# Fast-scheme products added up in TensorE's banks, with ScalarE's copies between them, and block sums of eight weight pieces moved into the second pair's groups

## The chip, the cores and the metric

One core of a Trainium2 chip runs the whole kernel. The metric is the device time of one execution in microseconds. The engines are TensorE (PE), VectorE (DVE), ScalarE (ACT), GpSimd (POOL) and SyncE (SP), which here issues most DMAs. Each has its own queue, works through it in the order written, and waits on semaphores.

## The reference

```
xn = layernorm(x)                          # x: 8 x 512 tokens x 512
q, k, v = xn @ Wq.T + bq, xn @ Wk.T + bk, xn @ Wv.T + bv
ctx = (elu(q)+1) * cumsum((elu(k)+1) * v, over tokens) * 32**-0.5
s = ctx @ Wo.T + bo
u = fwht(xn * SU_ug) / 64                  # Walsh-Hadamard transform over 512
h = silu(u @ W_gate.T * sg) * (u @ W_up.T * su)     # 2048 wide
f = fwht(h * SU_dp) / 64 @ W_down.T * sd
out = x + s * silu(f)
```

## The kernel before

All matrices are split into an fp16 high and low half, and each product is made of three fp16 matmuls (high x high, high x low, low x high). The tokens come in 8 chunks of 512, worked on as 4 pairs of chunks. The weights of q, k, v, gate and up are cut into 22 pieces ("groups" g = 0 to 21): pieces 0 to 5 are K, V, Q, K, V, Q, then gate and up alternate. A group gives four tiles of 128x512: two blocks of output rows by the two chunks of the pair.

The first pair (p = 0) computes its tiles plainly, 12 matmuls each, while the other engines prepare the weights for the later pairs: `s_sums` (lines 1040 to 1043) and `s_low` (line 1053) on VectorE with `s_high` on ScalarE make the block sums S1 to S4 of a piece, GpSimd loads their blocks and stores them. `S_TILES` says after which tile of the first pair each piece's sums are made; the last three of the 22 are made between the first and the second pair. Down weights are transformed and stored in four slabs, the last in group 20.

Pairs 1 to 3 use a fast 2x2 scheme: 7 products of 6 matmuls in place of 8 (`group`, lines 1446 to 1457), each into a bank of its own. VectorE adds the banks to four tiles in SBUF with 7 additions (`add`, line 919), which begin from ScalarE's copy of the first product (`copy_p1`, line 660). The finished tiles are then used: for K and Q ScalarE makes exp and relu (lines 670, 673) and VectorE the feature (line 925), for Q also the context (line 949); V is multiplied and scanned by VectorE (lines 935, 940); gate gets a Silu (line 683); up is multiplied by it (line 958) and split into halves by ScalarE (`hidden_high`, line 690) and VectorE (`hidden_low`, line 967). SyncE loads each group's weights five loads ahead into a ring of 5 slots.

After the groups of a pair TensorE runs four down quads of 48 matmuls for each chunk (line 1522) and an out product of 48 (line 1553). Meanwhile VectorE takes the contexts' maxima (`ctx_absmax`, line 819), the next pair's layernorm statistics (line 829) once its tokens have been loaded over the freed tiles (`load_x`, which waits for the last `h_ready`), the normalised tokens (line 855, after GpSimd's rstd), splits the contexts (lines 997, 998) and makes the next pair's token sums and their halves (`x_sums`, `t_low`, line 898). The order is written out by hand on each engine:

```
# DVE, pairs 1 to 3
last_sums(p)
ctx_absmax(p)
ln_stats(p + 1); normalise_pair(p + 1)     # p < 3
ctx_scale(p); split_ctx(p, 0..7)
x_sums(p + 1, 0); t_low(p + 1, 0)          # p < 3
out_scale(); outputs(2 * p)
...
# PE, first out product of the pair, t == 0
pe.wait_ge(ctx_split, 8 * p + 8)
elif p < PAIRS - 1:
    pe.wait_ge(x_ready, 2 * p + 3 + cc)
```

## Time and profile before

| | |
|---|---|
| median of 3 runs | 1337.56 us (1337.24 to 1337.63) |
| profiled execution | 1335.45 us, its span 1333.6 us |
| granted TensorE clock | 0.999 of full speed (2.4 GHz) |
| TensorE busy | 1305.5 us, 98% of the span |
| VectorE busy | 1011.3 us, 76% |
| ScalarE busy | 457.8 us, 34% |
| GpSimd busy | 41.8 us, 3% |
| first pair | tiles to 298 us, down quads and out products to 406 us |
| groups of the later pairs | from 406, 715 and 1024 us, some 201 us each |

Busy time of TensorE counts matmuls that overlap once; its ends are modelled, so a small idle time can be hidden behind a matmul's end, and starts are the safer thing to count from. Times of single operations overlap in the same way on VectorE and ScalarE: the distance from start to start is shorter than the duration.

### The profile page before, as it was taken

What the parts mean: (1) busy time and instruction counts of PE and PEld (TensorE: products, weight loads), DVE (VectorE), ACT (ScalarE), POOL (GpSimd) and SP (SyncE); (2) the same over time, 40 slices, a digit from 0 to 9 for tenths busy, and PEclk for the clock granted to TensorE, in tenths of its full rate; (3) what the DMA queues carried; (4) which work ended last, traced back from release to release, by engine and by line L of the source; (5) the groups of instructions that cost most, each with busy time, mean ns of one, the idle gap of its engine ahead of it and who ended that gap; (6) DMA issues with size and microseconds to landing.
All of it is one profiled execution on the core that took longest, in us unless ns stands there. A gap on an engine that the chain in (4) does not pass through costs nothing. (4 is left out here: it accounts for less than half of the span.)

```text
span 1333.6 us, 16120 instructions
## 1 busy us (share of the span) xinstructions
PE 1305.5 (98%) x6100; PEld 597.9 (45%) x6100; DVE 1011.3 (76%) x1629; ACT 457.8 (34%) x683; POOL 41.8 (3%) x72
## 2 busy tenths in 40 slices
PE   5999999999999999999999999999999999999998
PEld 3444444444444444444444444444444444444443
DVE  6899999979648997777717998778734998778333
ACT  5945545541123443330113443332112433332000
POOL 0102000001000000000000000000000000000000
PEclk9999999999999999999999999999999999999999
DMA  9624555568264323325244323325244423323240
GB/s 375 246 79 166 198 212 198 180 254 293 94 236 158 127 97 124 127 99 186 97 156 158 127 98 124 126 101 184 95 158 142 143 100 121 127 107 115 95 126 32
DMA packets 47550, 199.39 MB, mean 150 GB/s; under 512 B 5105, under 2 KB 5361, under 8 KB 31985
## 3 DMA queue, kind: packets, MB, share of 16 engines
q1 hardware_dynamic: 41424, 176.87, 36.9%
q0 software_dynamic: 6048, 21.50, 4.4%
q8 instruction: 48, 0.79, 0.2%
q14 instruction: 30, 0.24, 0.1%
HBM read 153.26 MB, written 45.09 MB: 149 GB/s over the span
## 5 line engine op out<-in xcount | busy, mean ns | idle before, releaser
L1455 PE MATMUL bank<-xops,ring 128*128 128x512 f16 x2772 | 601.1, 380 | 3.2 <-DVE work L919 3.1
L1455 PEld LDWEIGHTS bank<-xops,ring 128*128 128x128 f16 x2772 | 269.4, 98 | 334.4 <-DVE work L919 11.3
L919 DVE TENSOR_TENSOR work<-bank,work 128x512 f32<-128x512 f32 x462 | 305.4, 685 | 91.5 <-PE bank L1455 83.9
L1522 PE MATMUL bank<-ring,h_all 128*128 128x512 f16 x1536 | 333.8, 379 | 0.6 <-DMA ring<-scr_d 0.6
L1370 PE MATMUL bank<-xops,ring 128*128 128x512 f16 x1056 | 237.2, 379 | 1.5 <-DVE xops L868 1.5
L1522 PEld LDWEIGHTS bank<-ring,h_all 128*128 128x128 f16 x1536 | 150.0, 98 | 180.9 <-DMA ring<-scr_d 1.1
L1370 PEld LDWEIGHTS bank<-xops,ring 128*128 128x128 f16 x1056 | 102.5, 98 | 140.4 <-issue 28.1
L690 ACT ACTIVATE h_all<-work 128x512 f16<-128x512 f32 x128 | 80.2, 627 | 204.3 <-DVE work L958 204.3
L1189 DVE TENSOR_TENSOR gate_g<-bank,row 128x512 f32<-128x512 f32 x32 | 21.4, 689 | 104.5 <-PE bank L1522 103.9
L740 ACT ACTIVATE gate_g<-gate_g 128x512 f32<-128x512 f32 x32 | 19.9, 630 | 202.9 <-DVE gate_g L1189 202.9
L967 DVE TENSOR_TENSOR h_all<-work,h_all 128x512 f16<-128x512 f32 x128 | 87.4, 685 | 0.4
L683 ACT ACTIVATE work<-work,gate_out 128x512 f32<-128x512 f32 x96 | 66.4, 715 | 54.4 <-DVE work L919 54.4
L1553 PE MATMUL bank<-ring,ctx 128*128 128x512 f16 x384 | 84.2, 379 | 0.4 <-DVE xops L898 0.2
L958 DVE SCALAR_TENSOR_TENSOR work<-work,up_out 128x512 f32<-128x512 f32 x96 | 71.3, 743 | 0.0
L670 ACT ACTIVATE work<-work,vec,i_attn 128x512 f32<-128x512 f32 x48 | 38.8, 808 | 75.9 <-DVE work L919 75.9
L1553 PEld LDWEIGHTS bank<-ring,ctx 128*128 128x128 f16 x384 | 37.4, 98 | 46.2 <-issue 1.3
L660 ACT ACTIVATE work<-bank 128x512 f32<-128x512 f32 x66 | 38.7, 586 | 56.1 <-PE bank L1455 55.9
L925 DVE SCALAR_TENSOR_TENSOR work<-work 128x512 f32<-128x512 f32 x64 | 44.1, 689 | 13.7 <-ACT work L673 12.6
L631 ACT ACTIVATE ring<-ring 128x1024 f16<-128x1024 f32 x16 | 16.9, 1053 | 81.1 <-DVE ring L1043 78.0
L573 ACT ACTIVATE work<-bank 128x512 f32<-128x512 f32 x6 | 3.6, 597 | 112.6 <-PE bank L1482 112.6
L940 DVE TENSOR_TENSOR_SCAN work<-work 128x512 f32<-128x512 f32 x32 | 39.2, 1224 | 1.1
L673 ACT ACTIVATE work<-work,vec,i_attn 128x512 f32<-128x512 f32 x48 | 38.3, 799 | 0.0
(158 smaller groups left out, 835.6 us busy)
## 6 DMA issues: line engine op xcount, KB each, us to landing
ring<-scr_g SPq DMA_DIRECT2D x66, 1024.0 KB, 4.8
ring<-scr_d SPq DMA_DIRECT2D x32, 1024.0 KB, 4.8
scr_g<-ring SPq DMA_DIRECT2D x22, 512.0 KB, 3.5
scr_g<-ring POOLq DMA_DIRECT2D x22, 512.0 KB, 3.5
h_all<-in_ug_t SPq DMA_DIRECT2D x8, 1024.0 KB, 13.9
ring<-scr_f POOLq DMA_DIRECT2D x16, 512.0 KB, 3.7
x_res<-in_x SPq DMA_DIRECT2D x32, 256.0 KB, 3.5
out<-x_res SPq DMA_DIRECT2D x32, 256.0 KB, 6.8
```

Of the source, the lines that this page charges most:

```text
L670: act.activation(exp_tile(n), src, ACT.Exp, bias=vec[:, b + f:b + f + 1], scale=i_attn[:, m:m + 1])
L683: act.activation(tile(g, j), src, ACT.Silu, scale=gate_out[:, at:at + 1]).then_inc(act_tiles, 1)
L690: act.activation(h[:, i, TILE_OF[j], HI, :], tile(g, j), ACT.Copy).then_inc(h_hi, 1)
L919: dve.tensor_tensor(tile(g, to), bank[product][:, :], tile(g, other), ALU.add).then_inc(summed, 1)
L925: dve.scalar_tensor_tensor(tile(g, j), exp_tile(n), 1.0, tile(g, j), ALU.min, ALU.add) \
L940: dve.tensor_tensor_scan(tile(g, j), tile(g, j), tile(g, j), 0.0, ALU.add, ALU.bypass) \
L958: dve.scalar_tensor_tensor(tile(g, j), src, up_out[:, at:at + 1], tile(g - 1, j), ALU.mult, ALU.mult).then_inc(h_made, 1)
L967: dve.tensor_tensor(at[:, LO, :], tile(g, j), at[:, HI, :], ALU.subtract).then_inc(h_ready, 1)
L1370: mm = pe.matmul(plain_bank(g, j)[:, :], at[:, s, 2 * dh + kk, r, :], xops[:, kk, xs, PLAIN_B[dh][c], :], start=(n == 0), stop=(n == len(t ...
L1455: mm = pe.matmul(bank[n][:, :], weight_of(slot, s, b, kk), xops[:, kk, xs, c, :], start=(a == 0), stop=(a == 5))
L1522: mm = pe.matmul(bank[D_BANK[t]][:, :], at[:, s, cols], w[:, :, ws, :], start=(a == 0 and b == 0 and n == 0), stop=(a == KB - 1 and b == K ...
L1553: mm = pe.matmul(bank[R_BANK[t]][:, :], at[:, s, cols], o_weight(slot)[:, f, ws, :], start=(n == 0), stop=(n == 3 * KB - 1))
```

## The change

In pairs 1 to 3 the products of a group that belong to one sum are added by TensorE itself, because it goes on writing to the same bank. P1, P6, P7 and P4 go one after another into a "chain" bank; after each of the first three ScalarE copies the partial sum to a tile (`copy_sum`), and after the fourth the bank holds tile C21, which its user reads from the bank. P5 and then P3 share a "left" bank, P2 has a "right" bank. VectorE adds 3 times (`add`), one copy and one bank each. TensorE's order is interleaved over neighbouring groups (`group_order`), and in the last group of a pair 24 matmuls of the first down quad come ahead of the last two products and 24 behind them.

The tiles' order in a group is now C11, C22, C21, C12, and chunks, rows and plain banks of the first pair are renumbered with it. The block sums of pieces 14 to 21 are made in groups 6 to 13 of the second pair (`late_sums`; GpSimd loads and stores them, in a part of `h_all` that is free then); the first pair makes 14 at other tiles of its order.

```diff
 S1, S2, S3, S4, A11, A12, A22 = range(7)
-PRODUCTS = ((A11, B11), (S2, T2), (S3, T3), (S1, T1), (A12, B21), (S4, B22), (A22, T4))
+P1, P6, P7, P4, P5, P3, P2 = range(7)
+FACTORS = ((A11, B11), (S2, T2), (S3, T3), (A22, T4), (S1, T1), (S4, B22), (A12, B21))
+CHAIN_BANKS, LEFT_BANKS, RIGHT_BANKS = (0, 1), (2, 3), (4, 5)
...
+S_TILES = (2, 6, 10) + tuple(4 * g + 1 for g in range(8, 19))
 S_EARLY = len(S_TILES)
+S_LATE_FROM = 6
...
+def group_order(g):
+
+    if g == 0:
+        return [(0, P1), (0, P2), (0, P6), (0, P5), (0, P7), (1, P1)]
+    head = [(g - 1, P4), (g, P6), (g - 1, P3), (g, P2), (g, P7)]
+    if g < GROUPS - 1:
+        return head + [(g + 1, P1), (g, P5)]
+    return head + [(g, P5), (g, P4), (g, P3)]
+
+
+ORDER = [at for g in range(GROUPS) for at in group_order(g)]
+
+
+def products_to(p, g, m):
+
+    return len(ORDER) * (p - 1) + ORDER.index((g, m)) + 1
+
+def late_sums(g):
+
+    n = S_EARLY + g - S_LATE_FROM
+    return n if S_EARLY <= n < GROUPS else None
...
-            eng.wait_ge(summed, 7 * nth(p, g) + (3, 5, 6, 7)[j])
+            if j == C21:
+                eng.wait_ge(product_done, products_to(p, g, P4))
+                return chain_bank(g)[:, :]
+            eng.wait_ge(summed, 3 * nth(p, g) + (1, 2, 0, 3)[j])
...
-                    sp.wait_ge(product_done, 7 * nth(p, n) + 7)
+                    sp.wait_ge(product_done, products_to(p, n, P3))
...
-                    sp.wait_ge(s_stored, 16 * GROUPS)
+                    sp.wait_ge(s_stored, 16 * S_EARLY)
                     for s in range(3):
                         sp.wait_ge(piece_stored[s], 16 * len(range(s, GROUPS, 3)))
+                if p == 1 and S_EARLY <= n < GROUPS:
+                    sp.wait_ge(s_stored, 16 * (n + 1))
...
-                if n > S_OWN:
+                if n == S_EARLY:
+                    pool.wait_ge(quad_done, 2 * KB)
+                elif n > S_OWN:
                     pool.wait_ge(s_summed, n)
...
-                if n == S_EARLY + 1:
                     rstd_of(1)
+                    load_blocks(S_EARLY)
...
-            def copy_p1(p, g):
-
-                act.wait_ge(product_done, 7 * nth(p, g) + 1)
-                wait_free(act, p, g, SEED_TILE)
-                act.activation(tile(g, SEED_TILE), bank[0][:, :], ACT.Copy).then_inc(p1_copied, 1)
+            def copy_sum(p, g, n):
+
+                j = (C11, C12, C22)[n]
+                act.wait_ge(product_done, products_to(p, g, (P1, P6, P7)[n]))
+                wait_free(act, p, g, j)
+                act.activation(tile(g, j), chain_bank(g)[:, :], ACT.Copy).then_inc(copied, 1)
...
             def group(p, g):
+                if g == 0:
+                    copy_sum(p, g, 0)
+                elif kind_of(g - 1) != IS_UP:
+                    take(p, g - 1, C22)
+                copy_sum(p, g, 1)
+                if g and kind_of(g - 1) == IS_UP:
+                    take(p, g - 1, C22)
                 if g:
-                    take(p, g - 1, 2)
-                copy_p1(p, g)
+                    take(p, g - 1, C21)
+                copy_sum(p, g, 2)
+                if g + 1 < GROUPS:
+                    copy_sum(p, g + 1, 0)
+                if p == 1 and late_sums(g - 1) is not None:
+                    s_high(late_sums(g - 1))
                 if g:
-                    take(p, g - 1, 3)
-                take(p, g, 0)
-                take(p, g, 1)
+                    take(p, g - 1, C12)
+                take(p, g, C11)
...
-            s_high(S_EARLY)
             o_high()
-            s_high(S_EARLY + 1)
             silu_outs(0)
             x_high(1, 0)
             t_high(1, 0)
-            s_high(S_EARLY + 2)
...
+            def add(p, g, j):
+
+                at, m = ((right_bank(g), P2), (left_bank(g), P5), None, (left_bank(g), P3))[j]
+                dve.wait_ge(product_done, products_to(p, g, m))
+                dve.wait_ge(copied, 3 * nth(p, g) + (1, 3, 0, 2)[j])
+                dve.tensor_tensor(tile(g, j), at[:, :], tile(g, j), ALU.add).then_inc(summed, 1)
...
             def group(p, g):
                 if g:
-                    add(p, g - 1, 6)
-                    use(p, g - 1, 2)
-                    hidden_low(p, g - 1, 1)
-                add(p, g, 0)
+                    use(p, g - 1, C22)
+                    hidden_low(p, g - 1, C11)
+                    use(p, g - 1, C21)
+                    hidden_low(p, g - 1, C22)
+                    add(p, g - 1, C12)
+                add(p, g, C11)
                 if g:
-                    use(p, g - 1, 3)
-                    hidden_low(p, g - 1, 2)
-                add(p, g, 1)
+                    use(p, g - 1, C12)
+                    hidden_low(p, g - 1, C21)
+                add(p, g, C22)
                 if g:
-                    hidden_low(p, g - 1, 3)
-                add(p, g, 2)
-                add(p, g, 3)
-                add(p, g, 4)
-                use(p, g, 0)
-                add(p, g, 5)
-                use(p, g, 1)
-                hidden_low(p, g, 0)
+                    hidden_low(p, g - 1, C12)
+                use(p, g, C11)
+                if p == 1 and late_sums(g - 1) is not None:
+                    s_low(late_sums(g - 1))
+                if p == 1 and late_sums(g) is not None:
+                    s_sums(late_sums(g))
 
             def last_sums(p):
-                add(p, GROUPS - 1, 6)
-                use(p, GROUPS - 1, 2)
-                hidden_low(p, GROUPS - 1, 1)
-                use(p, GROUPS - 1, 3)
-                hidden_low(p, GROUPS - 1, 2)
-                hidden_low(p, GROUPS - 1, 3)
+                g = GROUPS - 1
+                use(p, g, C22)
+                hidden_low(p, g, C11)
+                use(p, g, C21)
+                hidden_low(p, g, C22)
+                add(p, g, C12)
+                use(p, g, C12)
+                hidden_low(p, g, C21)
+                hidden_low(p, g, C12)
...
-            s_sums(S_EARLY)
...
-            s_sums(S_EARLY + 1)
             for n in range(4, 8):
...
+            def wait_bank(p, g, m):
+
+                if m == P1:
+                    if g >= 2:
+                        wait_taken(pe, p, g - 2, C21)
+                    else:
+                        pe.wait_ge(z_ready, 8 * p - 4 + (2, 3)[g])
+                elif m in (P6, P7, P4):
+                    pe.wait_ge(copied, 3 * nth(p, g) + (P6, P7, P4).index(m) + 1)
+                elif m == P5:
+                    if g >= 2:
+                        pe.wait_ge(summed, 3 * nth(p, g - 2) + 3)
+                    elif g == 1:
+                        pe.wait_ge(o_read, 8 * p - 4 + 1)
+                    else:
+                        pe.wait_ge(z_ready, 8 * p - 4 + 4)
+                elif m == P3:
+                    pe.wait_ge(summed, 3 * nth(p, g) + 2)
+                elif g >= 2:
+                    pe.wait_ge(summed, 3 * nth(p, g - 2) + 1)
+                else:
+                    pe.wait_ge(o_read, 8 * p - 4 + (2, 3)[g])
+
+            def product(p, g, m):
+                slot = slot_of(p, g)
+                if m == P1:
+                    pe.wait_ge(slot_loaded[slot], 16 * loads_into(p, g))
+                    if g == 0:
+                        pe.wait_ge(x_ready, 2 * p + 2)
+                wait_bank(p, g, m)
+                to = chain_bank(g) if m in (P1, P6, P7, P4) else right_bank(g) if m == P2 else left_bank(g)
+                b, c = FACTORS[m]
+                terms = [(kk, s, xs) for kk in range(2) for s, xs in ((HI, HI), (HI, LO), (LO, HI))]
+                for a, (kk, s, xs) in enumerate(terms):
+                    mm = pe.matmul(to[:, :], weight_of(slot, s, b, kk), xops[:, kk, xs, c, :],
+                                   start=(a == 0 and m in (P1, P2, P5)), stop=(a == 5),
+                                   skip_group_check=True)
...
+            def group(p, g):
 
                 if g == 0:
-                    if n < 3:
-                        pe.wait_ge(z_ready, 8 * p - 4 + n + 2)
-                    else:
-                        pe.wait_ge(o_read, 8 * p - 4 + n - 2)
-                elif n == 0:
-                    pe.wait_ge(p1_copied, nth(p, g))
+                    product(p, 0, P1)
+                    product(p, 0, P2)
+                    product(p, 0, P6)
+                    product(p, 0, P5)
+                    product(p, 0, P7)
                 else:
-                    pe.wait_ge(summed, 7 * nth(p, g - 1) + (1, 2, 4, 5, 6, 7)[n - 1])
-
-            def group(p, g):
-                slot = slot_of(p, g)
-                pe.wait_ge(slot_loaded[slot], 16 * loads_into(p, g))
-                if g == 0:
-                    pe.wait_ge(x_ready, 2 * p + 2)
-                for n, (b, c) in enumerate(PRODUCTS):
-                    wait_bank(p, g, n)
-                    terms = [(kk, s, xs) for kk in range(2) for s, xs in ((HI, HI), (HI, LO), (LO, HI))]
-                    for a, (kk, s, xs) in enumerate(terms):
-                        mm = pe.matmul(bank[n][:, :], weight_of(slot, s, b, kk), xops[:, kk, xs, c, :],
-                                       start=(a == 0), stop=(a == 5))
-                    mm.then_inc(product_done, 1)
+                    product(p, g - 1, P4)
+                    product(p, g, P6)
+                    product(p, g - 1, P3)
+                    product(p, g, P2)
+                    product(p, g, P7)
+                if g + 1 < GROUPS:
+                    product(p, g + 1, P1)
+                if g:
+                    product(p, g, P5)
+                if g + 1 == GROUPS:
+                    down_part(2 * p, 0, (0, 1))
+                    product(p, g, P4)
+                    product(p, g, P3)
+                    down_part(2 * p, 0, (2, 3))
...
-                    pe.wait_ge(summed, 7 * nth(p, GROUPS - 1) + t - 1)
-
-            def down_quad(c, a):
+                elif t == 0:
+                    pe.wait_ge(z_ready, 4 * c - 3)
+                elif t < 3:
+                    wait_taken(pe, p, GROUPS - 3 + t, C21)
+                else:
+                    pe.wait_ge(summed, 3 * nth(p, GROUPS - 2) + 3)
...
                 for a in range(KB):
-                    down_quad(2 * p, a)
+                    if a or not p:
+                        down_quad(2 * p, a)
                     if a == 2 and 0 < p < PAIRS - 1:
                         transposes(p + 1, 0)
```

## Rows read from the trace of the kernel before

**Rows 1.** The chain that ended last, in order of time: start us, us, what.
```profile
1276.83 41.44 PE bank L1522 x192
```

**Rows 2.** Each pair's groups (two of three): stretch, its length, busy by engine.
```profile
406.13:607.30 201.17, 200.21 (x926) 89.81 (x925) 167.04 (x255) 77.45 (x117) 0.00 (x0) 1.00 0.36 126
714.68:916.20 201.52, 200.20 (x926) 89.81 (x925) 167.03 (x255) 77.44 (x117) 0.00 (x0) 1.00 0.35 126
```

**Rows 3.** Timeline of TensorE, second pair, group 6: start us, us, engine, line.
```profile
778.75 2.55 PE L1455 MATMUL bank<-xops,ring 128*128 128x512 f16 x11 [0.51 <-DVE work L919]
```

**Rows 4.** TensorE's waits in the first pair: us in total, times, longest.
```profile
PE bank L1522 <- DMA ring<-scr_d: 0.6, 1, 0.6
```

**Rows 5.** Groups of VectorE in the first of these stretches: busy, mean ns, idle before.
```profile
L919 DVE TENSOR_TENSOR work<-bank,work 128x512 f32<-128x512 f32 x153 | 101.1, 685 | 30.4 <-PE bank L1455 28.0 <-issue 1.5
```

**Rows 6.** Groups of VectorE in the first pair, shapes apart.
```profile
L1053 DVE TENSOR_TENSOR ring<-ring 128x1024 f16<-128x1024 f32 x13 | 15.8, 1219 | 0.1
...
L1043 DVE TENSOR_TENSOR ring<-ring 128x256 f32<-128x256 f32 x16 | 6.8, 425 | 0.5
```

**Rows 7.** Timeline of TensorE, first product of a pair.
```profile
406.13 2.11 PE L1455 MATMUL bank<-xops,ring 128*128 128x512 f16 x9
```

**Rows 8.** Timeline of ScalarE, first groups of the same pair.
```profile
407.62 0.60 ACT L660 ACTIVATE work<-bank 128x512 f32<-128x512 f32 x1 [3.61 <-PE bank L1455]
408.24 1.28 ACT L670 ACT_TABLE_LOAD   x1
...
416.69 0.60 ACT L660 ACTIVATE work<-bank 128x512 f32<-128x512 f32 x1
417.18 0.80 ACT L670 ACTIVATE work<-work,vec,i_attn 128x512 f32<-128x512 f32 x1
417.89 0.80 ACT L673 ACTIVATE work<-work,vec,i_attn 128x512 f32<-128x512 f32 x1
```

**Rows 9.** Timeline of VectorE, group 5 (three additions, then V's tiles).
```profile
451.48 1.89 DVE L919 TENSOR_TENSOR work<-bank,work 128x512 f32<-128x512 f32 x3
...
455.78 0.74 DVE L935 SCALAR_TENSOR_TENSOR work<-work,bv_in 128x512 f32<-128x512 f32 x1
...
457.70 0.67 DVE L919 TENSOR_TENSOR work<-bank,work 128x512 f32<-128x512 f32 x1
```

**Rows 10.** Timeline of VectorE, Q's tiles.
```profile
465.73 0.69 DVE L925 SCALAR_TENSOR_TENSOR work<-work 128x512 f32<-128x512 f32 x1 [0.39 <-ACT work L673]
...
467.13 0.68 DVE L919 TENSOR_TENSOR work<-bank,work 128x512 f32<-128x512 f32 x1
```

**Rows 11.** Timeline at the end of that pair's groups, VectorE then ScalarE.
```profile
608.67 0.74 DVE L958 SCALAR_TENSOR_TENSOR work<-work,up_out 128x512 f32<-128x512 f32 x1
...
609.45 0.63 ACT L690 ACTIVATE h_all<-work 128x512 f16<-128x512 f32 x1 [1.23 <-DVE work L958]
```

**Rows 12.** Timeline of ScalarE in the first pair, first gate group.
```profile
98.66 1.28 ACT L683 ACT_TABLE_LOAD   x1
99.95 1.50 ACT L683 ACTIVATE work<-bank,gate_out 128x512 f32<-128x512 f32 x2
```

**Rows 13.** Timeline at the end of that pair's groups.
```profile
607.30 12.90 PE L1522 MATMUL bank<-ring,h_all 128*128 128x512 f16 x59
...
611.99 4.83 DVE L819 TENSOR_REDUCE ctx_max<-ctx 128x1 f32<-128x512 f32 x8
...
617.58 2.47 DVE L829 BATCH_NORM_STATS2 stats<-work 128x6 f32<-128x512 f32 x4 [0.57 <-DMA work<-in_x]
```

**Rows 14.** Timeline at that pair's first out product.
```profile
648.27 2.36 DVE L898 TENSOR_TENSOR xops<-work,xops 128x1024 f16<-128x1024 f32 x2 [1.45 <-ACT xops L580]
...
650.77 4.48 PE L1553 MATMUL bank<-ring,ctx 128*128 128x512 f16 x20
```

**Rows 15.** Timeline of TensorE, the next pair's first out product.
```profile
959.79 1.46 PE L1553 MATMUL bank<-ring,ctx 128*128 128x512 f16 x6 [0.24 <-DVE xops L898]
```

**Rows 16.** Timeline of VectorE between rows 13 and 14.
```profile
627.57 0.17 DVE L852 TENSOR_SCALAR rstd<-rstd 128x8 f32<-128x8 f32 x1 [3.99 <-POOL rstd L485]
```

More of the change, by code:

```diff
@@ L81 @@
 DOWN_HIGH_AT, DOWN_LOW_AT = 14, 15
-S_TILES = (2, 6, 10) + tuple(4 * g + 1 for g in range(6, GROUPS))
+S_TILES = (2, 6, 10) + tuple(4 * g + 1 for g in range(8, 19))
 S_EARLY = len(S_TILES)
+S_LATE_FROM = 6
 S_OWN = 3
@@ L300, in plain_bank, with chain_bank, left_bank, right_bank @@
             return bank[PLAIN_BANKS[(4 * g + j) % len(PLAIN_BANKS)]]
+        def chain_bank(g):
+            return bank[CHAIN_BANKS[g % 2]]
+        def left_bank(g):
+            return bank[LEFT_BANKS[g % 2]]
+        def right_bank(g):
+            return bank[RIGHT_BANKS[g % 2]]
         def wait_taken(eng, p, g, j):
@@ L768, in _ @@
                     group(p, g)
-                take(p, GROUPS - 1, 2)
-                take(p, GROUPS - 1, 3)
+                for j in (C22, C21, C12):
+                    take(p, GROUPS - 1, j)
                 if p < PAIRS - 1:
@@ L1509, in down_quad @@
                 pe.wait_ge(slot_loaded[slot], 16 * loads)
[L1510 to L1525 removed]
+                for b in range(KB):
+                    k = KB * QUADS[a] + b
+                    i, r = k % 8, k // 8
+                    if cc == 0:
+                        pe.wait_ge(h_ready, 32 * p + 4 * i + 4)
+                    w, at = quad(slot)[:, :, b, :, :], h[:, i, 2 * r + cc, :, :]
+                    for t in ts:
+                        if a == 0 and b == 0:
+                            wait_down_bank(c, t)
+                        cols = slice(t * P, (t + 1) * P)
+                        for n, (s, ws) in enumerate(((HI, HI), (HI, LO), (LO, HI))):
+                            mm = pe.matmul(bank[D_BANK[t]][:, :], at[:, s, cols], w[:, :, ws, :],
+                                           start=(a == 0 and b == 0 and n == 0),
+                                           stop=(a == KB - 1 and b == KB - 1 and n == 2))
+                if ts[-1] == TB - 1:
+                    mm.then_inc(quad_done, 1)
+            def down_quad(c, a):
+                for ts in ((0, 1), (2, 3)) if a == 0 else ((0, 1, 2, 3),):
+                    down_part(c, a, ts)
             def out_product(c, t):
```

114 lines of the change are left out of this document (42 added, 72 removed).

## The prediction

> **What bounds the kernel now.** I read the page's busy shares first (the table above: TensorE nearly all of the span), then the chain that ended last. The chain's late part is TensorE alone, with 192 matmuls of 128x512 in 41.44 us [rows 1], so one takes 0.2158 us and one product of the fast scheme (6 matmuls) T = 1.295 us. The second view is the stretch of each pair's groups [rows 2]: 22 groups of 42 matmuls are 924 x 0.2158 = 199.43 us, and the stretches last 201.17, 201.52 and, in the last pair, as long as the first of them. So TensorE loses 1.74 + 2.09 + 1.74 = 5.6 us in all in the groups; the reader should see how small this is. Its timeline puts the losses in group 6, where TensorE waits for VectorE's additions of line 919 [rows 3]. That is where VectorE's debt from pieces 4 (V) and 5 (Q) comes due. In the first pair, from which the change takes block sums, TensorE's wait at the end is 0.6 us before the first down quad, and it is for a DMA, not for VectorE [rows 4]. The third place is the end of each pair, below.
>
> **What is removed.** Per group 7 additions become 3: 66 x 4 = 264 of 0.685 us [rows 5], 181 us of VectorE. It lies beside TensorE, except for the 5.6 us above. Eight block sums (four operations of 0.42 us, one of 1.22 us each [rows 6]) leave the first pair and the passage to the second. TensorE waits for none of them, so this is worth nothing: cover is TensorE's own work, and the 0.6 us before the quads hangs on the fourth down slab, whose stores follow its own tiles. In the second pair's groups 6 to 14 they cost VectorE 1.7 + 1.2 = 2.9 us a group. A gate group needs only its 3 additions (2.1 us), an up group 3 additions, 4 products of 0.74 and 4 subtractions (under 8 us), so the two average under 8 of 9.06 us, and the tightest point (the bank of C21, needed 5 T = 6.5 us into a group) just holds: 0.20 + addition 0.60 + product 0.66 + 1.13 + 1.6 of late sums + product 0.66 + subtraction 0.60 + product 0.74 = 6.2. Cost 0; if that cover is missing, about 0.3 us in each of four up groups. The pieces are stored some three groups before their loads; SyncE's new waits pass.
>
> **What is added: loops inside the groups.** The matmul count is the same, so TensorE's cost is only waits. Its order is now, per group g: P4(g-1), P6(g), P3(g-1), P2(g), P7(g), P1(g+1), P5(g). Each sum in a bank is copied by ScalarE before the next product goes on it, with two products (2.59 us) of cover. I walk the queues with these steps:
> - a product can be read 0.20 us after its slot ends (start 406.13, + 1.295, copy starts 407.62) [rows 7, 8];
> - ScalarE: copy to next 0.49, exp to relu 0.71, relu 0.80, exp+relu to the next 1.42; a table load 1.28 [rows 8];
> - VectorE: an addition or a plain product 0.69, but the next can start after 0.60 (three take 1.89); V's multiply and scan 1.92 together, the multiply alone 0.74 [rows 9]; Q's feature and context 1.40 together [rows 10];
> - a hand-over between engines 0.03 to 0.05 (608.67 + 0.74 = 609.41, and the copy starts at 609.45) [rows 11].
>
> K groups: ScalarE takes tile C12 of g-1 only after copying P1(g+1); VectorE adds C22 of g only after using that tile; P3(g) waits for it, due 3 T = 3.89 us after P1(g+1). The loop is 0.20 + 0.49 + 0.71 + 0.80 + 0.03 + 0.60 + 0.69 + 0.05 = 3.57: no loss.
> Q groups: the same with 1.40 for 0.60, that is 4.37: loss 0.48, twice a pair.
> V groups: VectorE's part starts at 2.23 of that loop (up to the feature), then 0.60 + 0.60 + 2 x 1.92 + 0.74 + 0.05 = 8.06 until C21 is taken from the bank; P1 of the group after next is due at 6 T = 7.77: loss 0.29, twice a pair.
> Group 1: ScalarE now copies P1(1) ahead of the pair's first exp, and the table load before that exp begins at 6 T + 0.20 + 0.60 = 8.57 us, after this copy, where it used to lie in an idle stretch. 8.57 + 1.28 + two tiles of 1.42 = 12.70, copy of P6(1) done at 13.33 with its hand-over; P7(1) is due at 10 T = 12.95: loss 0.38.
> Gate and up groups: copies come 1.3 to 1.8 us before need; no loss.
> Sum 0.38 + 2 x 0.48 + 2 x 0.29 = 1.9 a pair, 5.8 in all, against 5.6 now: **+0.2 us**. The debt that VectorE had goes, and ScalarE's place in the loops brings about as much back. Bounds: nothing (each wait hidden; -5.6) and twice my losses (+6.0); I take the walk, since each of its steps is a row.
>
> Whether more than the 1.28 us lies between a load and the work behind it shows in the first pair's first gate group: the load starts at 98.66 and the Silu at 99.95 [rows 12], so nothing follows. The Trainium skill (ScalarE: Activation LUTs, What ACT_TABLE_LOAD costs) says otherwise, a drain of about 1.38 us on top, 2.66 in all; by it group 1 would lose 1.76 instead of 0.38 us, and this sum would be 4.1 us higher. The trace does not agree with it.
>
> **What is moved: the end of each pair.** P4 and P3 of group 21 now come behind 24 matmuls of the first down quad. The last product thus ends 4 T = 5.18 us after the point E where the groups used to end, instead of at E. VectorE still goes through all of the last group's tiles before it starts the contexts' maxima (line 819), the next pair's statistics and the rest. Before: E = 607.30, maxima from 611.99, which is E + 4.69 [rows 13]. After: 5.18 + 0.20, the addition of C12 0.72, its product 0.74, hand-over 0.04, ScalarE's half 0.63 [rows 11], 0.03, and 0.60 to the next: E + 8.14. **3.45 us later.**
> Who waits for that? In the second and third pair VectorE makes the next pair's tokens (line 898) before TensorE may start the out product of line 1553. That chain is already what ends last: line 898 ends at 648.27 + 2.36 = 650.63 and line 1553 starts at 650.77 [rows 14]; one pair later the profile names line 898 as what TensorE waited for [rows 15]. Between the maxima and there VectorE has 38 us of work with two waits: 0.57 for the tokens' landing [rows 13] and 3.99 for GpSimd's rstd [rows 16]. Both move along, because the load is issued when the last hidden tile is done and rstd needs the statistics. So the delay arrives whole: 2 x 3.45 = **+6.9 us**. The last pair has no next tokens: its out product needs only split contexts, which would be ready near E + 25 and are due at E + 41.4, so 0. Bounds: 0, if those waits (4.6 us) swallowed it all, and 3.45 + 1.0 a pair, if the tokens' load, now closer behind the load of the out weights, landed 1 us later. I take 3.45.
> Starts of pairs: P2(0) now needs the second out tile read 1.3 us in instead of 5.2; VectorE reads it before the pair's first product starts, between the out products of that chunk. Cost 0.
>
> **Sum.** +0.2 + 6.9 = +7.1 us. The profiled execution took 1335.45 (span 1333.6, 1.8 around it), which gives 1342.6; the median is 2.1 above it, so 1337.56 + 7.1 = **1344.7 us**, 0.5% slower. Within 0.2% (2.7 us) a measurement of this kernel can't tell from no change.
>
> **Rivals.**
> A, my forecast: 1344.7, by itself 1342 to 1347. Chance 0.68.
> B, more waits inside the groups: the late sums of the second pair, or hand-overs a little longer in the V and Q loops, double my losses: +6 gives up to 1350; half of it 1347.7. For: the margins are 0.2 to 0.3 us. Against: the steps are measured. 0.08.
> B2, the table load before the pair's first exp holds ScalarE for as long again as its row says (1.28 us): group 1 loses 1.28 more, 3.8 in three pairs, 1348.5. For: two loads of the groups stand ahead of an idle stretch, where this wouldn't show. Against: [rows 12]. 0.04. This is the skill's rule of that page, which would put it at 1348.8.
> C, the groups lose nothing while the pair's end does: -5.6 + 6.9 gives 1338.9, within 0.2%. For: the loops may start from work that ScalarE did earlier. Against: copy and take stand in one queue. 0.12.
> E, the reordered end costs nothing: 1337.8. Against: [rows 14, 15]. 0.03.
> D, faster: TensorE is fed without a wait through the groups (-5.6), from VectorE's freed 181 us. It decides once the pair's end costs under 1.4 us a pair instead of 3.45; with none it gives 1332.0. For: the two waits inside the chain are longer than the delay. Against: both begin with work that is itself late. 0.05.
>
> **Chances and range.** Slower A + B + B2: 0.80; same C + E: 0.15; faster D: 0.05. The range takes in C's time and B's lower half: 1338.8 to 1348.0.
>
> **What the changed profile would show.** Right: additions x198, copies x198; TensorE's groups of pair 1 in about 201.3 us plus the 24 matmuls, with waits of 0.3 to 0.5 us for VectorE in groups 1 to 6 and none in group 6's old places; the maxima starting 8.1 us after E; the first out product of the second and third pair waiting 3.7 us for line 898's successor; none in the last pair; first pair unchanged to 0.2 us. Wrong: no wait ahead of those out products (then E or D), or groups above 203 us (B). Most dangerous for me are margins of tenths in the V and Q loops, and the assumption that VectorE's order at the pair's end has no slack.

## The result and the profile after

The changed kernel took 1351.94 us (median of 4 runs, 1349.76 to 1352.52), the kernel before beside it 1337.40 (1336.52 to 1337.63). The ratio is 1.0107 with a 95% interval of [1.0089, 1.0124]: 1.1% slower, some 14.5 us, where 7.1 us were forecast. The direction was right, the size was not, and 1351.94 lies above the range of 1338.8 to 1348.0. The profiled execution took 1349.76 us (span 1347.9), 14.3 us more than the one before.

The page gives the sizes. The additions fell to 198 and the copies rose to 198, as the diff says, and VectorE went from 76% to 63% of the span. TensorE's busy time rose by 5.6 us with the same 6100 matmuls, which waits alone don't explain. Columns of the groups: busy, mean ns of one, then the idle time before them and its releaser.
```profile
PE 1311.1 (97%) x6100; PEld 599.5 (44%) x6100; DVE 853.2 (63%) x1365; ACT 528.6 (39%) x815; POOL 46.6 (3%) x72
...
L972 DVE TENSOR_TENSOR work<-bank,work 128x512 f32<-128x512 f32 x198 | 134.2, 687 | 181.9 <-PE bank L1519 167.3
...
L1648 PE MATMUL bank<-ring,ctx 128*128 128x512 f16 x384 | 88.6, 393 | 7.5 <-DVE xops L961 7.5
```

TensorE's waits by releaser (us in total, times, longest) name the places. Line 1648 is the out product (line 1553 before) and line 961 the halves of the next pair's tokens (line 898 before).
```profile
PE bank L1648 <- DVE xops L961: 7.5, 2, 3.8
PE bank L1519 <- DVE work L972: 1.9, 6, 0.3
...
PE bank L1519 <- DVE work L1011: 1.5, 2, 1.1
...
PE bank L1519 <- DVE work L988: 1.2, 6, 0.2
...
PE bank L1519 <- ACT work L716: 0.7, 3, 0.2
```

**The pair's end.** TensorE's timeline in the first of the two (start, length, line, count), then VectorE's. The products of line 1519 end when the next line starts, at 614.60; the point E of the forecast is 4 T = 5.18 us ahead of that, 609.42. The maxima (line 882) start at 617.68 = E + 8.26, where they started at E + 4.69 [rows 13]: 3.57 us later. Both waits inside the chain move along (0.61 and 3.87, before 0.57 and 3.99 [rows 13, 16]), line 961 ends at 656.31, and TensorE, which had nothing left to do, starts at 656.45. In the kernel before it started without such a wait [rows 14].
```profile
606.83 5.34 PE L1612 MATMUL bank<-ring,h_all 128*128 128x512 f16 x24
612.01 2.75 PE L1519 MATMUL bank<-xops,ring 128*128 128x512 f16 x12
614.60 7.72 PE L1612 MATMUL bank<-ring,h_all 128*128 128x512 f16 x35
...
648.72 4.05 PE L1612 MATMUL bank<-ring,h_all 128*128 128x512 f16 x18
656.45 7.84 PE L1648 MATMUL bank<-ring,ctx 128*128 128x512 f16 x23 [3.68 <-DVE xops L961]
```
```profile
617.68 4.83 DVE L882 TENSOR_REDUCE ctx_max<-ctx 128x1 f32<-128x512 f32 x8
...
626.03 2.47 DVE L892 BATCH_NORM_STATS2 stats<-work 128x6 f32<-128x512 f32 x4 [0.61 <-DMA work<-in_x]
...
633.25 0.17 DVE L915 TENSOR_SCALAR rstd<-rstd 128x8 f32<-128x8 f32 x1 [3.87 <-POOL rstd L538]
...
653.95 2.36 DVE L961 TENSOR_TENSOR xops<-work,xops 128x1024 f16<-128x1024 f32 x2 [1.45 <-ACT xops L635]
```

**What stands behind the wait.** The windows around it (stretch, length, busy by engine, granted clock, DMA share, GB/s) show what the forecast did not have. Around a wait of 3.7 us the granted clock falls to half, 1.2 GHz, where it was 1.00 (2.4 GHz) in the 10 us up to 650: 14 matmuls in 5 us instead of 23, then 2.4 GHz again. By their starts 12 matmuls stand 0.427 us behind the one before instead of 0.216, and one 0.38, which is 2.7 us lost. One pair later, behind a wait of 3.79 us, it is 7 such matmuls and 1.7 us.
```profile
655.00:657.00 2.00, 0.55 (x2) 0.29 (x3) 1.97 (x4) 0.00 (x0) 0.00 (x0) 0.54 0.95 401
657.00:662.00 5.00, 5.00 (x14) 1.72 (x12) 0.98 (x3) 1.23 (x2) 0.00 (x0) 0.50 0.01 3
662.00:665.00 3.00, 3.00 (x16) 1.35 (x15) 2.36 (x4) 0.63 (x1) 0.00 (x0) 1.00 0.01 3
...
970.00:972.00 2.00, 0.10 (x1) 0.13 (x2) 1.97 (x4) 0.00 (x0) 0.00 (x0) 1.00 0.95 397
972.00:977.00 5.00, 5.00 (x16) 1.90 (x15) 1.83 (x3) 1.23 (x2) 0.00 (x0) 0.66 0.03 13
```
The Trainium skill (TensorE: Matmul & The Clock Gate, What's actually happening) says that the array's clock is gated to half after a stretch without work and let go by activity. The trace agrees, with the 0.50 behind the wait and the 1.00 that follows.

The fall does not coincide with the wait. The first time the clock is down before TensorE starts again at 656.45 (0.54 in the window from 655). The second time it is still at 1.00 up to 972.00, when TensorE has been working again since 971.90, and falls behind that.

**The groups.** From here on a wait is the distance between the starts of two matmuls beyond 0.216 us, worked out from the trace. Each pair loses 0.41 + 0.12 in group 1, 0.37 twice in the V groups and 0.49 twice in the Q groups, 2.25 us. The second pair loses 2.0 more around the late sums, 1.28 at 503.7 and 0.60 at 523.1. Together 8.8 us, against 5.5 in the same count of the trace before. (The row at 778.75 us in [rows 3] is of the third pair; the second has the like at 467 and 469 us.) In the second pair the groups take 609.42 - 405.73 = 203.7 us, above the 203 that the forecast had named as the sign of rival B.

ScalarE in group 1: the table load starts right behind the copy of P1(1), and TensorE waits until the copy at 418.46, as walked.
```profile
413.70 0.60 ACT L716 ACTIVATE work<-bank 128x512 f32<-128x512 f32 x1 [0.70 <-PE bank L1519]
414.32 1.28 ACT L726 ACT_TABLE_LOAD   x1
415.61 0.82 ACT L726 ACTIVATE work<-work,vec,i_attn 128x512 f32<-128x512 f32 x1
...
418.46 0.58 ACT L716 ACTIVATE work<-bank 128x512 f32<-128x512 f32 x1
```
```profile
405.73 13.11 PE L1519 MATMUL bank<-xops,ring 128*128 128x512 f16 x60
419.09 10.65 PE L1519 MATMUL bank<-xops,ring 128*128 128x512 f16 x48 [0.24 <-ACT work L716]
```

VectorE at the late sums of the second pair. It comes to them (line 1094) at 500.10 and stands until 501.32, because the piece's block has not landed. Its product of line 1011, which reads C21 from the bank, thus starts at 504.28 and ends at 505.02, and TensorE's next product waits for it until 505.17.
```profile
498.88 1.22 DVE L1107 TENSOR_TENSOR h_all<-h_all 128x1024 f16<-128x1024 f32 x1
501.32 0.42 DVE L1094 TENSOR_TENSOR h_all<-h_all 128x256 f32<-128x256 f32 x1 [1.22 <-DMA h_all<-scr_f]
...
504.28 0.74 DVE L1011 SCALAR_TENSOR_TENSOR work<-bank,up_out,work 128x512 f32<-128x512 f32 x1
```
```profile
505.17 18.29 PE L1519 MATMUL bank<-xops,ring 128*128 128x512 f16 x84 [1.12 <-DVE work L1011]
```
GpSimd issues this block's load at 493.26, only when the sums before it have read the shared buffer, and it lands 8.04 us later. The DMA issues from 455 to 545 us (KB each, median us to landing) give 6.9 us for such a load, beside ten loads of 1 MB by SyncE. In the first pair of the kernel before (120 to 200 us) the same 512 KB took 3.5 us. That SyncE's loads are the reason is likely, but no run tests it.
```profile
ring<-scr_g SPq DMA_DIRECT2D x10, 1024.0 KB, 6.3
h_all<-scr_f POOLq DMA_DIRECT2D x7, 512.0 KB, 6.9
```

**The balance** of the two profiled executions: groups +3.3 (8.8 less 5.5); out products +7.1 (3.85 + 3.96 less the 0.29 + 0.41 of before); half clock behind them +4.4 (2.7 + 1.7); start of the groups 0.4 earlier. The sum is +14.4, the spans differ by 14.3. Of the 0.4 the wait for the last down slab explains all: TensorE waited 0.58 us for it before and 0.18 now.

### The profile page after: what moved, and what is told of

Same layout as the page of the kernel before. It is cut to its first block, busy times and chain, and to the rows that moved or that the text cites. A ratio compares the mean times of both kernels' runs of the same rounds, so it can differ in the third digit from the quotient of the medians.

```text
span 1347.9 us, 16024 instructions
## 1 busy us (share of the span) xinstructions
PE 1311.1 (97%) x6100; PEld 599.5 (44%) x6100; DVE 853.2 (63%) x1365; ACT 528.6 (39%) x815; POOL 46.6 (3%) x72
## 4 chain that ended last, share of the span: by engine, by line
PE 77%; DVE 9%; ACT 4%; DMA 4%; issue 4%; SPq 0%; POOL 0%; DVEq 0%; ACTq 0%
PE bank L1519 35%; PE bank L1612 19%; PE bank L1421 13%; PE bank L1648 6%; PE bank L1454 2%; DMA h_all<-scr_f 2%; DMA work<-in_x 2%; ACT work L726 1%; ACT work L729 1%; PE bank L1465 1%; DVE work L988 1%; DVE ctx L1051 1%; DVE work L972 1%; DVE work L978 1%; DVE work L918 1%
## 5 line engine op out<-in xcount | busy, mean ns | idle before, releaser
L972 DVE TENSOR_TENSOR work<-bank,work 128x512 f32<-128x512 f32 x198 | 134.2, 687 | 181.9 <-PE bank L1519 167.3
L716 ACT ACTIVATE work<-bank 128x512 f32<-128x512 f32 x198 | 118.0, 596 | 244.8 <-PE bank L1519 244.8
L1648 PE MATMUL bank<-ring,ctx 128*128 128x512 f16 x384 | 88.6, 393 | 7.5 <-DVE xops L961 7.5
L1011 DVE SCALAR_TENSOR_TENSOR work<-bank,up_out,work 128x512 f32<-128x512 f32 x56 | 41.9, 748 | 24.6 <-PE bank L1519 11.4
L739 ACT ACTIVATE work<-work,gate_out 128x512 f32<-128x512 f32 x72 | 51.2, 717 | 5.4 <-DVE work L972 5.0
L1011 DVE SCALAR_TENSOR_TENSOR work<-work,up_out 128x512 f32<-128x512 f32 x72 | 51.9, 745 | 0.3
L628 ACT ACTIVATE work<-bank 128x512 f32<-128x512 f32 x6 | 3.6, 598 | 109.7 <-PE bank L1571 109.7
L739 ACT ACTIVATE work<-bank,gate_out 128x512 f32<-128x512 f32 x56 | 38.1, 681 | 21.2 <-PE bank L1421 21.1
L1252 DVE SCALAR_TENSOR_TENSOR s_f<-bank,o_out,row 128x512 f32<-128x512 f32 x32 | 23.9, 748 | 18.1 <-PE bank L1648 18.1
```

What stands on the lines that cost most here:

```text
L716: act.activation(tile(g, j), chain_bank(g)[:, :], ACT.Copy).then_inc(copied, 1)
L739: act.activation(tile(g, j), src, ACT.Silu, scale=gate_out[:, at:at + 1]).then_inc(act_tiles, 1)
L972: dve.tensor_tensor(tile(g, j), at[:, :], tile(g, j), ALU.add).then_inc(summed, 1)
L1011: dve.scalar_tensor_tensor(tile(g, j), src, up_out[:, at:at + 1], tile(g - 1, j), ALU.mult, ALU.mult).then_inc(h_made, 1)
L1648: mm = pe.matmul(bank[R_BANK[t]][:, :], at[:, s, cols], o_weight(slot)[:, f, ws, :], start=(n == 0), stop=(n == 3 * KB - 1))
```

## The experiments

Each was run beside the kernel before on the same chip; waits are of the profiled execution. e1 to e4 share one chip and its runs of the kernel before (1336.85, 13 runs), e6 to e9 another (1337.21, 9 runs).

One thing makes single executions differ, and it is no part of any edit. At 70 us, in the first pair, TensorE waits 1.9 to 2.5 us for VectorE in every trace. In those of e1, e2, e3, e4 and e8 some matmuls behind this wait run at half clock, in the others none do: from 73 to 78 us e8 has 13 matmuls at a mean granted clock of 0.67, e7 has 21 at 1.00, behind the same wait of 2.49 us. The groups of the second pair start at 406.9 to 408.8 us in the five, at 405.7 to 406.1 in the others (407.2 in e9, for a reason given there). So times within a trace are compared from the start or the end of its groups, and a single execution can lie 1 to 2 us off for this alone.

**e1_end_order**: the changed kernel with only the last group's order put back.
```diff
                 if g + 1 == GROUPS:
-                    down_part(2 * p, 0, (0, 1))
                     product(p, g, P4)
                     product(p, g, P3)
+                    down_part(2 * p, 0, (0, 1))
                     down_part(2 * p, 0, (2, 3))
```


> The changed kernel with P4 and P3 of group 21 right behind P5, both halves of the first down quad after them. Theory (the moved products hold VectorE up by 3.45 us, so TensorE stands 3.8 us before two out products, and its clock falls to half behind each): both waits go, no clock at half speed, 12 us less than the changed kernel, near 1339.7. Rival 1 (the half clock has its cause elsewhere, in the new order of the groups): waits go, half clock stays, near 1344. Rival 2 (the waits come from late tokens, from the closer load of the out weights): waits stay, no gain.

Measured 1337.07 us (1336.07 to 1338.08), ratio 1.0003 [0.9994, 1.0013]. Moving 24 matmuls past two products accounts for the whole loss. VectorE's and TensorE's timelines: the groups end at 609.83 and the maxima start 4.37 us behind that, where they started 8.26 us behind E; line 961 ends at 652.74, and line 1648 follows the down quads with no wait. No matmul there is at half clock.
```profile
614.20 4.83 DVE L882 TENSOR_REDUCE ctx_max<-ctx 128x1 f32<-128x512 f32 x8
...
650.38 2.36 DVE L961 TENSOR_TENSOR xops<-work,xops 128x1024 f16<-128x1024 f32 x2 [1.45 <-ACT xops L635]
```
```profile
653.01 3.19 PE L1648 MATMUL bank<-ring,ctx 128*128 128x512 f16 x14
```
The rest of the change, with group waits of 7.4 us against 5.5, is worth nothing that these runs can measure.

**e3_before_late_end**: the opposite, the moved matmuls alone in the kernel before (its down quad is split into parts as in the change).
```diff
                 for n, (b, c) in enumerate(PRODUCTS):
+                    if g == GROUPS - 1 and n == 5:
+                        down_part(2 * p, 0, (0, 1))
                     wait_bank(p, g, n)
...
                     mm.then_inc(product_done, 1)
+                if g == GROUPS - 1:
+                    down_part(2 * p, 0, (2, 3))
...
-                    down_quad(2 * p, a)
+                    if a or not p:
+                        down_quad(2 * p, a)
```


> The kernel before with only the moved end: 24 matmuls of the first down quad ahead of its last two products. Theory: the maxima start 4.6 us later than before (9.3 us after the old end of the groups), TensorE waits 4.9 us before two out products, the clock is at half speed after each: 9.2 us for the waits and 4 to 6 for the clock, 1350 to 1353. Rival 1 (half clock comes from something else in the changed kernel): 1346.6. Rival 2 (the groups' sums in the banks are what costs): 1338.

Measured 1353.20 us (1350.87 to 1354.60), ratio 1.0121 [1.0104, 1.0138]. One part of the change alone gives more than the whole loss. The waits were 5.89 and 5.66 us (longer than the 4.9 expected; here an addition and three tiles also lie behind the last two products, which may be the reason), and 25 matmuls ran at half clock, 5.3 us. Waits less before's 0.7 and the clock make +16.1; the medians differ by 16.4. The spans of the two profiled executions differ by 19.2, because in this one the groups also start 2.7 us later, the half clock in the first pair being one of the reasons. TensorE's timeline, then the windows:
```profile
659.08 6.09 PE L1561 MATMUL bank<-ring,ctx 128*128 128x512 f16 x15 [5.73 <-DVE xops L898]
```
```profile
659.00:664.00 5.00, 4.92 (x12) 1.75 (x13) 1.35 (x3) 1.23 (x2) 0.00 (x0) 0.50 0.00 0
```

**e2_two_raw**: the late sums get a second buffer for the loaded block, so that GpSimd loads one piece ahead.
```diff
-            return half_slot(3 + a) if n < S_EARLY else h_late[:, 2048 * a:2048 * a + 2048]
+            if n < S_EARLY:
+                return half_slot(3 + a)
+            part = 3 if a == 0 and (n - S_EARLY) % 2 else a
+            return h_late[:, 2048 * part:2048 * part + 2048]
...
+                elif n > S_EARLY:
+                    pool.wait_ge(s_summed, n - 1)
...
-                        .then_inc(s_loaded, 16)
+                        .then_inc(s_loaded if n < S_EARLY else s_late[(n - S_EARLY) % 2], 16)
```


> The changed kernel with two buffers for the blocks of the late sums, so each load is issued one group earlier. Theory (VectorE stands 1.2 and 0.6 us for a load that takes 6.9 us and was issued only after the previous sums, and hands the bank of C21 over late): the TensorE waits of 1.28 and 0.60 us in groups 10 and 12 of the second pair go, 1.9 us less, near 1350. Rival (the late sums' own 2.9 us a group on VectorE are too much in an up group): waits stay at 0.3 us or more in each up group.

Measured 1348.77 us (1347.83 to 1349.23), ratio 1.0089 [1.0074, 1.0104]. VectorE's timeline shows the sums (now line 1102) starting right behind line 1115 of the piece before, with no wait for the block (each buffer has a semaphore of its own for its loads):
```profile
499.97 1.22 DVE L1115 TENSOR_TENSOR h_all<-h_all 128x1024 f16<-128x1024 f32 x1
501.29 0.43 DVE L1102 TENSOR_TENSOR h_all<-h_all 128x256 f32<-128x256 f32 x1
```
TensorE's two waits there became 0.17 and 0.07 us. The mechanism is thus right, but its size is loose: the same code of the late sums cost TensorE 0.8 us in all in e1, 1.1 in e4 and e5 and 1.3 in e6, against 2.0 in the changed kernel and 0.4 here. The ratio's interval overlaps that of the changed kernel.

**e4_loops**: for K, V, Q and gate tiles ScalarE takes C12 ahead of its second copy, and VectorE adds C12 ahead of using C21.
```diff
+                if g and kind_of(g - 1) != IS_UP:
+                    take(p, g - 1, C12)
                 copy_sum(p, g, 2)
...
-                if g:
+                if g and kind_of(g - 1) == IS_UP:
                     take(p, g - 1, C12)
...
+                    if kind_of(g - 1) != IS_UP:
+                        add(p, g - 1, C12)
                     use(p, g - 1, C21)
                     hidden_low(p, g - 1, C22)
-                    add(p, g - 1, C12)
+                    if kind_of(g - 1) == IS_UP:
+                        add(p, g - 1, C12)
```


> The changed kernel, where for K, V, Q and gate groups VectorE adds C12 before it uses C21, and ScalarE takes C12 before it copies the sum after P7 (up groups as they were). Theory (two loops through ScalarE's and VectorE's order cost 0.49 us per Q group and 0.37 per V group): those four waits a pair go, 5.2 us less, near 1346.7; the 0.53 us of group 1 stay. Rival (TensorE waits because sums in a bank can't be read at once): the same waits at the same places, 1351.9.

Measured 1345.82 us (1344.28 to 1347.12), ratio 1.0067 [1.0052, 1.0082]. The V and Q waits are gone from all pairs, those of group 1 stay: behind the one at 420.60 TensorE's timeline has 275 matmuls in one piece.
```profile
420.60 59.64 PE L1524 MATMUL bank<-xops,ring 128*128 128x512 f16 x275 [0.23 <-ACT work L716]
```
The out products still waited 4.31 and 4.59 us, with 17 matmuls at half clock.

**e5_table** (one execution, no interval): an exp of one column at the start of a pair, so that the table is loaded in ScalarE's idle stretch.
```diff
                 if g == 0:
+                    act.wait_ge(halves_set, 1)
+                    act.activation(spare[:, 0:1], minus_half[:, 0:1], ACT.Exp)
                     copy_sum(p, g, 0)
```


> The changed kernel with only the one-column Exp ahead of each pair's first copy. Theory (the table load behind the copy of P1 of group 1 makes the copy of P6 late): the waits of 0.41 and 0.12 us in group 1 of each pair go, all others stay; some 1.6 us less, which one time can't show, so the waits in the trace decide. Rival (group 1 waits for the adding of the first group's tiles): the waits stay.

It took 1346.91 us beside 1338.53 for the kernel before. ScalarE's timeline shows the load moved from 414.32 to 403.85 and the first exp right behind the copy; TensorE's shows group 1 without a wait, as far as the first V group. That held in all three pairs.
```profile
403.85 1.28 ACT L788 ACT_TABLE_LOAD   x1
405.15 0.20 ACT L788 ACTIVATE spare<-minus_half 128x1 f32<-128x1 f32 x1
...
413.92 0.60 ACT L717 ACTIVATE work<-bank 128x512 f32<-128x512 f32 x1 [0.70 <-PE bank L1522]
414.41 0.80 ACT L727 ACTIVATE work<-work,vec,i_attn 128x512 f32<-128x512 f32 x1
```
```profile
405.94 23.47 PE L1522 MATMUL bank<-xops,ring 128*128 128x512 f16 x108
429.62 10.74 PE L1522 MATMUL bank<-xops,ring 128*128 128x512 f16 x49 [0.20 <-DVE work L991]
```
Here and in the changed kernel the instruction behind a table load starts 0.01 to 0.02 us after it ends (414.32 + 1.28, then 415.61), so rival B2 is out.
The Trainium skill (ScalarE: Activation LUTs, What ACT_TABLE_LOAD costs) adds a drain to each load; neither of these traces has one behind it or ahead of it (the copy ahead ends at 414.30, the load starts at 414.32).

**e6_half**: 12 of the 24 matmuls ahead of the last two products in place of 24.
```diff
-                    down_part(2 * p, 0, (0, 1))
+                    down_part(2 * p, 0, (0,))
                     product(p, g, P4)
                     product(p, g, P3)
+                    down_part(2 * p, 0, (1,))
                     down_part(2 * p, 0, (2, 3))
```


> The changed kernel with 12 instead of 24 matmuls of the first down quad ahead of the last two products. Theory (a wait at each out product that grows one for one with the delay, and a fall of the clock only behind a long wait): the waits shrink by 2.6 us each to about 1.2 us, and no matmul behind them runs at half speed: 5.2 for the waits and 4 or more for the clock, near 1342. Rival (the clock falls after any wait there, in proportion): half of the loss, near 1344.5, with some half-speed matmuls left.

Measured 1342.51 us (1339.93 to 1343.84), ratio 1.0038 [1.0025, 1.0052]. The waits were 1.75 and 1.50 us; in the profiled execution (1339.93, mean granted clock 1.000) no matmul behind them was at half clock. The other three had mean clocks of 1.000, 0.997 and 0.996 and spans of 1339.5, 1342.0 and 1342.0 us. So the clock probably fell in two of them; they have no trace that could show the place, and the wait at 70 us is as good a candidate as those before the out products.
```profile
653.58 6.63 PE L1649 MATMUL bank<-ring,ctx 128*128 128x512 f16 x30 [1.59 <-DVE xops L961]
```
```profile
653.00:658.00 5.00, 4.42 (x21) 2.08 (x22) 3.41 (x7) 1.23 (x2) 0.00 (x0) 1.00 0.55 210
```

**e8_before_half_end**: the same halved step in the kernel before, to get a wait between those of e6 and of the changed kernel. The diff is against e3.
```diff
                     if g == GROUPS - 1 and n == 5:
-                        down_part(2 * p, 0, (0, 1))
+                        down_part(2 * p, 0, (0,))
...
                 if g == GROUPS - 1:
+                    down_part(2 * p, 0, (1,))
                     down_part(2 * p, 0, (2, 3))
```


> The kernel before with 12 matmuls of the down quad ahead of its last two products. Theory: waits of 2.3 to 2.6 us before two out products, 4.4 more than before. If such a wait is too short to lower the clock, 1341.3; if it is long enough, half-speed matmuls behind it and 1344 to 1346.

Measured 1345.08 us (1344.67 to 1346.29), ratio 1.0063 [1.0048, 1.0078]. The waits were 3.01 and 3.40 us. Behind the shorter one 7 matmuls ran at half clock, behind the longer one none. Windows of the two:
```profile
655.50:659.00 3.50, 3.50 (x12) 1.40 (x11) 1.16 (x2) 1.23 (x2) 0.00 (x0) 0.66 0.34 143
...
968.80:972.50 3.70, 3.45 (x17) 1.59 (x17) 2.18 (x5) 1.23 (x2) 0.00 (x0) 1.00 0.31 128
```

All out-product waits with what stood behind them, worked out from the starts of the matmuls (at half clock means some 0.43 us behind the one before):

| kernel | waits, us | matmuls at half clock |
|---|---|---|
| before, e1, e7, e9 | up to 0.4 | 0 |
| e6 | 1.75, 1.50 | 0, 0 |
| e8 | 3.01, 3.40 | 7, 0 |
| the changed kernel | 3.85, 3.96 | 12, 7 |
| e2 | 4.13, 4.83 | 12 in all |
| e5 | 3.92, 4.22 | 15 in all |
| e4 | 4.31, 4.59 | 17 in all |
| e3 | 5.89, 5.66 | 25 in all |

**e7_all**: the changed kernel with e1, e2, e4 and e5 together.

> The changed kernel with all four repairs: the last two products ahead of the down quad, two buffers for the late blocks, C12 added and taken earlier for groups that are not up, and a one-column Exp ahead of the pair's first copy, so that the table load lies in ScalarE's idle stretch. Theory: the waits in the groups fall from 7.2 us (with the end repaired) to under 0.5, those before the out products stay 0; 6 to 7 us less than with the end repaired alone, about 1330.5, 0.45 to 0.5% faster than the kernel before. Rival (the repairs overlap, or a next loop of the same size lies right behind): waits of 0.1 to 0.3 us a group remain, 1334.

Measured 1330.93 us (1329.35 to 1331.34), ratio 0.9951 [0.9939, 0.9964], so 6.3 us faster than the kernel before. Its group waits are 0.84 us in all, one of them 0.64 at 501.7, behind a block whose load took 8.65 us (issued at 490.00) and for which VectorE stood 0.57 us. TensorE's timeline shows that one wait, and the passage to the out product without any:
```profile
406.00 96.06 PE L1535 MATMUL bank<-xops,ring 128*128 128x512 f16 x444
502.53 103.89 PE L1535 MATMUL bank<-xops,ring 128*128 128x512 f16 x480 [0.47 <-DVE work L1022]
...
639.09 10.52 PE L1628 MATMUL bank<-ring,h_all 128*128 128x512 f16 x48
649.45 10.52 PE L1664 MATMUL bank<-ring,ctx 128*128 128x512 f16 x48
```

**e9_all_early_sums** (the diff is against e7): e7 with five of the eight moved block sums back in the first pair, at their old places; the last three stay in the second pair's groups.
```diff
-S_TILES = (2, 6, 10) + tuple(4 * g + 1 for g in range(8, 19))
+S_TILES = (2, 6, 10) + tuple(4 * g + 1 for g in range(6, GROUPS))
...
-                elif n in (3, 7, 11):
-                    down_bound((n + 1) // 4)
+                elif n in (5, 9, 13):
+                    down_bound((n - 1) // 4)
```


> As the run with all four repairs, but with 19 pieces' block sums in the first pair at their old places and only the last three in the second pair's groups. Theory (the first pair's VectorE work is hidden behind TensorE): the same time as with all four repairs within 0.5 us. Rival (taking five pieces' sums out of the first pair makes it shorter): 1 us or more slower than that run.

Measured 1330.33 us (1329.45 to 1332.49), ratio 0.9951 [0.9939, 0.9964], the same as e7. The groups lose 0.07 us; TensorE's timeline has 924 matmuls, a whole pair of groups, in one piece:
```profile
407.19 199.66 PE L1535 MATMUL bank<-xops,ring 128*128 128x512 f16 x924
```
The two profiles show why. In e9 TensorE waits 0.9 us for the last down slab ahead of the first down quad, in e7 0.2; the groups start at 407.19 and 406.00 (the other 0.5 us is there before 200 us). Moving the five pieces saves TensorE some 0.7 us in the first pair and costs it 0.8 in the groups, and in the total nothing is left that these runs can measure. The last three pieces, which the kernel before sums between the first and the second pair, are not tested by it.

## Why the prediction was too low

Right, point by point:
- **The end of the pair.** +6.9 was forecast for two waits, +7.1 measured; 3.7 us was named for each, 3.85 and 3.96 came. VectorE's delay was 3.57 us against 3.45, and it arrived whole. e1 and e3 show it from both sides: undone, it takes the loss away, done alone, it makes all of it.
- **Where the groups wait.** ScalarE's place in the K, Q and V loops and the table load ahead of the first exp, at the places walked; the gate and up groups without late sums lose nothing. e4 removes the first kind and e5 the second, and each leaves the other kind in place.
- **The first pair** and the passage to the second: nearly no gain from taking eight sums out, 0.4 us here. The reason given was not quite right, though: the wait of 0.6 us for the fourth down slab was said to hang on its own stores alone, and it is 0.2 us in the changed kernel, 0.2 in e7 and 0.9 in e9.

Wrong, the largest first:
- **A term was missing: half clock behind the two waits, 4.4 us.** This is the step that failed. The sum turned 2 x 3.45 us of waiting into 6.9 us of time and let the matmuls behind each wait run as before, without giving a reason. The trace before had no wait of such a length in the later pairs, and behind the one of 2.0 us in its first pair the clock stayed at 1.00, so no row showed it; the term would have needed a case of its own. It should have been a rival with a chance, between nothing and, by what came behind the first wait, 2 x 2.7 us. Waits of 3.9 us cost some 6 us each in the changed kernel.
- **The late sums were costed at nothing and cost 2.0 us** in the profiled execution. The step that failed is "the tightest point just holds: 6.2" against 6.5. It counted VectorE's instructions and took the block as landed. The block came 1.2 us late, which is four times the margin of 0.3. This was rival B, and the 0.3 in each of four up groups that the working gave for lost cover was too small as well.
- **The loops were 0.33 us a pair too short**: 2.25 against 1.92. Q's 0.49 was right (0.48); V's was 0.37 for 0.29, group 1's 0.53 for 0.38. Steps of tenths add up to such an error; over three pairs it is 1.0 us.

These three make 7.4 us, and the forecast fell 7.2 short, by the medians and by the profiled executions (1349.76 against 1342.6).

Rival D, faster, was given 0.05, with 1332.0 if the pair's end cost nothing and the groups did not wait. Its two conditions are what e7 and e9 set up, and they came in at 1330.9 and 1330.3. By the profiled executions that is traced: e7's span is 5.5 us shorter than that of the kernel before, 4.7 from the groups, 0.7 from the waits of 0.29 and 0.41 us ahead of before's out products, which D's sum had left out, and 0.1 from an earlier start. The medians on that chip differ by 6.3; the 0.8 between is not placed. So with the additions in the banks the groups can run with hardly a wait, and the order around them hid it. Whether a new order alone could do the same for the kernel before, whose VectorE has more to do, was not tried.

What stays open: why the clock fell behind a wait of 3.01 us and not behind one of 3.40. And the changed kernel's other three runs lie 1.8 to 2.8 us above its profiled one. They have no trace; their mean granted clocks are lower (0.994 and 0.995 against 0.996), so more time at half clock, at 70 us or elsewhere, is the likely reason.

## What to carry to other kernels

When a step is moved behind other TensorE work, follow its result through every engine to the next thing that TensorE waits for: 24 matmuls put ahead of two products add no matmul and still cost 14 us. Price a wait of TensorE of some us as the wait and, as a case with its own chance, the matmuls behind it at half clock (here 1.3 to 2.9 us more where it fell). An engine with 158 us less to do (VectorE here) gives nothing unless the places where its results are waited for move earlier, and a margin of 0.3 us is no cover when a DMA lands in it.

## What the runs showed of the hardware

- The length of a wait did not decide alone whether the granted clock fell: 3.01 us was followed by 7 matmuls at 0.427 us, 3.40 us by none, and 3.85 and 3.96 us in one execution by 12 and 7. At 5.7 to 5.9 us it fell both times, with 25 matmuls in all.
- Shorter waits were followed by it too. Behind a wait of 2.4 to 2.5 us at 70 us, which eight traces have, it fell in five (e1 to e4, e8) and not in three (e5, e7, e9); behind 1.9 to 2.1 us, in the three others, it did not.
- It fell during one wait and behind others: in the changed kernel the clock was down before TensorE started again in the second pair, and went down after it had started again in the third.
- A 512 KB load issued by GpSimd landed in 3.5 us in the first pair and in 6.9 us (changed kernel) and 8.0 us (e7), all medians, beside SyncE's 1 MB loads of the groups, although the DMA engines carried about the same in both stretches, 204 and 199 GB/s.
- A load of an activation table took 1.28 us each time, and nothing followed it: where work stood ready, the next instruction started 0.01 to 0.02 us after its end.
